# Two attentions and two mixtures of experts on one core: smaller matmul tiles in the first attention, and another way for the gates of the last experts

## The reference

```python
x = layernorm(x + attn0(x))   # causal, scores clipped to [-10, 10], softmax
x = layernorm(x + ffn0(x))    # 8 experts of 256, top 2, silu(x W1) * (x W2) @ W3
x = layernorm(x + attn1(x))   # full attention with rotary q and k, bias on the output
x = layernorm(x + ffn1(x))    # 4 experts of 512, top 2 of softmax(gelu(x rW1) rW2)
# ffn1, the "last experts":
for e in range(4):
    h = gelu((x * mask_e) @ We1[e] + be1[e])
    out += (h @ We2[e] + be2[e]) * weight_e
```

## Time and profile before

| | |
|---|---|
| median of 3 runs | 1720.16 us (1710.94 to 1721.71) |
| profiled execution | 1729.45 us, its span 1727.2 us |
| mean granted TensorE clock | 0.953 of full speed |
| busy: PE, DVE, ACT, POOL | 1566.1, 1410.2, 1167.6, 108.6 us |
| first attention | about 54 to 345 us |
| first experts | about 369 to 744 us |
| second attention | about 790 to 1404 us |
| last experts | about 1428 to 1727 us |

### The profile page before, as it was taken

The page is one execution under the profiler, slowest core; times in us unless marked ns, Lnnn a source line. Parts: engine busy times, 40 slices in busy tenths (PEclk is TensorE's granted clock), DMA queues, the critical chain, the costliest instruction groups (busy, mean ns, idle before and its releaser), DMA issues.

```text
span 1727.2 us, 32148 instructions
## 1 busy us (share of the span) xinstructions
PE 1566.1 (91%) x11104; PEld 801.1 (46%) x11104; DVE 1410.2 (82%) x2503; ACT 1167.6 (68%) x1779; POOL 108.6 (6%) x187
## 2 busy tenths in 40 slices
PE   6899999969999999968999999999999978888887
PEld 3433333346656655633333333333333336666665
DVE  3688999867777777777999999999999827887777
ACT  3798999833333333215999999999999966655565
POOL 2000000000100111020000000000000000010000
PEclk9898999989999999975999999999999989999999
DMA  7482222222322221240111111111111010000100
GB/s 214 146 234 85 91 91 92 69 69 63 100 100 91 71 83 62 91 154 3 44 38 48 54 37 38 37 43 37 42 54 43 18 39 14 20 21 26 34 7 13
DMA packets 68461, 112.97 MB, mean 65 GB/s; under 512 B 23088, under 2 KB 32176, under 8 KB 67712
## 3 DMA queue, kind: packets, MB, share of 16 engines
q1 hardware_dynamic: 68352, 111.48, 20.6%
HBM read 67.79 MB, written 43.65 MB: 65 GB/s over the span
## 4 chain that ended last, share of the span: by engine, by line
PE 57%; DVE 19%; issue 9%; ACT 6%; DMA 4%; SPq 3%; POOL 1%; ACTq 0%; DVEq 0%; POOLq 0%
PE full_o L731 14%; PE max_pair L702 11%; PE causal_o L459 6%; PE hid_pair L1028 6%; PE triple L443 6%; PE score L716 3%; DVE negmax_h L816 3%; PE bank L1119 2%; DVE hid L1435 2%; DVE lin_u L1431 2%; ACT cprobs L487 1%; PE bank L1131 1%; DMA k_scr<-qk_hi 1%; DVE st L1263 1%; PE hid_pair L960 1%
## 5 line engine op out<-in xcount | busy, mean ns | idle before, releaser
L816 DVE TENSOR_REDUCE negmax_h<-max_pair 128x2 f32<-128x1024 f32 x512 | 588.3, 1217 | 23.4 <-PE max_pair L702 23.3
L782 ACT ACTIVATE probs<-score 128x512 f32<-128x512 f32 x1024 | 547.2, 596 | 78.6 <-PE score L716 59.2
L731 PE MATMUL full_o<-probs,v_st 128*32 128x256 f32 x4096 | 330.8, 395 | 17.7 <-ACT o_sb L790 17.7
L716 PE MATMUL score<-q_st,k_st 32*128 32x512 f32 x1024 | 316.6, 503 | 0.8 <-ACT probs L782 0.7
L487 ACT ACTIVATE cprobs<-triple 128x1536 f32<-128x1536 f32 x192 | 265.7, 1454 | 22.6 <-PE triple L443 19.9
L702 PE MATMUL max_pair<-k_st,q_st 32*128 32x512 f32 x1024 | 264.2, 515 | 10.9 <-DVE negmax_h L816 9.6
L1225 ACT ACTIVATE act_s<-hid_pair 128x512 f32<-128x512 f32 x128 | 76.5, 597 | 192.6 <-PE hid_pair L1028 192.5
L702 PEld LDWEIGHTS max_pair<-k_st,q_st 32*128 32x128 f32 x1024 | 97.6, 188 | 234.4 <-DVE negmax_h L816 179.9
L1028 PE MATMUL hid_pair<-x_hi,w_hi 128*128 128x512 f32 x384 | 198.8, 518 | 6.8 <-ACT act_s L1230 6.8
L517 DVE TENSOR_SCALAR cprobs<-cprobs 128x1536 f32<-128x1536 f32 (+6 forms) x272 | 163.5, 625 | 0.4 <-ACT cprobs L487 0.4
L459 PE MATMUL causal_o<-cprobs,v_st 128*32 128x512 f32 (+3 forms) x1536 | 157.6, 507 | 3.2 <-DVE cprobs L517 3.2
(11 more groups left out here) (139 smaller groups left out, 1631.4 us busy)
## 6 DMA issues: line engine op xcount, KB each, us to landing
o_scr<-o_sb SPq DMA_DIRECT2D x64, 256.0 KB, 2.1
gate_all<-gate_scr SPq DMA_DIRECT2D x32, 512.0 KB, 5.6
k_st<-k_scr SPq DMA_DIRECT2D x64, 128.0 KB, 2.8
q_st<-q_scr SPq DMA_DIRECT2D x128, 64.0 KB, 2.4
q_st<-q_scr SPq DMA_DIRECT2D x16, 512.0 KB
k_st<-k_scr SPq DMA_DIRECT2D x64, 104.0 KB
q_scr<-qk_hi SPq DMA_DIRECT2D x24, 256.0 KB, 4.1
k_scr<-qk_hi SPq DMA_DIRECT2D x24, 256.0 KB, 4.2
```

Of the source, the lines that this page charges most:

```text
L716: nc.tensor.matmul(sbank[L.score_bank(e)][:, :], k_st[p][rows, j, kt * P:(kt + 1) * P], q_st[p][rows, q0:q0 + w], start=True, stop=True, t ...
L731: last = nc.tensor.matmul(full_o[SLOT * j:SLOT * (j + 1), cols], v_st[p][:, kt, j, :], probs[s % NP][:, j, cols], start=(kt == 0 and part ...
L782: nc.scalar.activation(probs[s % NP][:, L.HEADS[j], :], sbank[L.score_bank(e)][:, :], ACT.Exp, scale=SCALE).then_inc(L.exp_done, 1)
L816: nc.vector.tensor_reduce(negmax_h[:, qt // TPC, half, heads[0]:heads[1] + 1:2, qt % TPC], ring[slot][:, :, :], AXX, ALU.max, negate=True) ...
```

## The change

- First attention: the keys lie in `k_st[128, T]`, 32 rows for each head, and a score matmul reads 32 rows (`slot_rows`). No zeros are needed. The "twins" pieces pair two key tiles of one head and stand behind key block 0 of the second half, so at most two blocks end in one slot. The first half's output is saved at slot 7, not 5.
- Weights: `w_hi` and `w_lo` have memory of their own and GpSimd makes them, one instruction of 2048 columns a round, in rounds 10 to 13 of the first attention and 2 to 5 of the second. SP loads the weights in rounds 5, 6 and 8 of the first attention, and those of the last experts in the first round of the second. The pad rows are gone; GpSimd fills the two extra key rows with ones by a memset, and fills `v_st`.
- The second attention reads 24 rows (maxima) and 26 rows (scores) of a head. Its first two rounds are loaded during the first experts (chunks 2 and 3).
- Last experts: the gates go to DRAM and back as in the first experts, and are turned in step 2 of their own chunk. Bank 1 becomes the second `y_bank`, and four hidden banks are used. GpSimd makes the router's exponential as a power of e (`pool_gate_exp`, 16 columns), and takes the chunk ahead first. `plan[1]` has other steps, and the first three hidden products stand ahead of the router's second product.
- SP's and GpSimd's loops are written out.

```diff
@@ -50,22 +50,24 @@
-    SAVE_PREV, SAVE_0 = 1, 5
+    SAVE_PREV, SAVE_0 = 1, 7
...
+        twins = [("twins", [(qc, qc * TPC + 2, j, 2 * P * qc, 2 * P) for qc in range(CPB)]) for j in self.HEADS]
         pieces = []
         for qc in range(CPB):
             d = qc * TPC
             for kt in range(d):
                 pieces += [("full", [(qc, kt, j, 0, CH)]) for j in self.HEADS]
+                if kt == 0:
+                    pieces += twins
             pieces += [("first", [(qc, d, j, 0, CH)]) for j in self.HEADS]
             pieces += [("edges", [(qc, d + 3, j, 0, P), (qc, d + 1, j, P, 3 * P)]) for j in self.HEADS]
-            pieces += [("twins", [(qc, d + 2, j, 0, 2 * P), (qc, d + 2, j + 1, 2 * P, 2 * P)]) for j in (0, 2)]
...
-        self.last_kt = [qc * TPC + 2 for qc in range(CPB)]
+        self.last_kt = [2, KT - 1]
...
-        def rows_of(j):
-
-            r = ROWS * (j * SLOT // ROWS)
-            return r, slice(r, r + ROWS)
+        def slot_rows(j, many):
+
+            return SLOT * j, slice(SLOT * j, SLOT * j + many)
...
-                r, rows = rows_of(j)
-                last = nc.tensor.matmul(triple[n % 2][:, bk, off:off + w], k_st[p][rows, j, kt * P:(kt + 1) * P],
+                r, rows = slot_rows(j, SLOT)
+                last = nc.tensor.matmul(triple[n % 2][:, bk, off:off + w], k_st[p][rows, kt * P:(kt + 1) * P],
                                         q_st[p][rows, q0:q0 + w], start=True, stop=True, tile_position=(r, 0))
...
+        def pool_round_weights(layer, k, lower):
+
+            if lower:
+                nc.gpsimd.tensor_tensor(w_lo[k][:, :], w_raw[k][:, :], w_hi[k][:, :].bitcast(F32),
+                                        ALU.subtract).then_inc(w_lower, 1)
+            else:
+                nc.gpsimd.tensor_copy(w_hi[k][:, :], w_raw[k][:, :]).then_inc(w_upper, 1)
+
+        def pool_weights(pool, layer, n):
+
+            k = n // 2
+            if n % 2 == 0:
+                pool.wait_ge(raw_loaded[k], 16 * (layer + 1))
+            else:
+                pool.wait_ge(w_upper, 2 * layer + k + 1)
+            pool_round_weights(layer, k, n % 2 == 1)
+
+        WEIGHTS_FROM = 10
...
+            for i in range(NG - 2):
+                pool.wait_ge(L.pv_done, L.values_before(i + 1))
+                pool_stage_v(pool, L, i + 2, i % 2)
+                if 0 <= i - WEIGHTS_FROM < 4:
+                    pool_weights(pool, 0, i - WEIGHTS_FROM)
+            pool.wait_ge(L.scores_ready, L.N * NG)
+            for p in range(2):
+                nc.gpsimd.memset(k_st[p][:, :].bitcast(F32), 1.0).then_inc(layers[1].ones_set, 1)
...
+            for i in range(4, NG - 2):
+                next_round(i, i % 2)
+                if i == 5:
+                    for t, name in WEIGHTS:
+                        sp.dma_start(t[tuple(slice(None) for _ in t.shape)], d[name]).then_inc(w_loaded, 16)
+                    sp.dma_start(b_o1[:, :], d["b_o1"].broadcast_to([P, D])).then_inc(w_loaded, 16)
+                    sp.dma_start(rb2[:, :], d["rb2"].broadcast_to([P, E1])).then_inc(w_loaded, 16)
+                if i == 6:
+                    for k, name in enumerate(("w1", "w2")):
+                        sp.dma_start(w_raw[k][:, :], d[name]).then_inc(raw_loaded[k], 16)
+                if i == 8:
+                    sp.dma_start(rope_a[:, :], d["rope_a"]).then_inc(rope_loaded, 16)
+                    sp.dma_start(rope_b[:, :], d["rope_b"]).then_inc(rope_loaded, 16)
...
+        def pool_fill_values(pool, L):
+
+            pool.wait_ge(stages[1].y_done, 2 * B * SPC)
             for p in range(2):
-                nc.gpsimd.memset(k_st[p][:, :, :].bitcast(F32), 0.0).then_inc(L.zeroed, 1)
+                nc.gpsimd.memset(v_st[p][:, :, :, :], 0.0).then_inc(fills, 1)
+            pool.wait_ge(fills, FILLS + 4 * L.n + 2)
+            for p in range(2):
+                nc.gpsimd.memset(v_st[p][:, :, :, DK:DK + 1], 1.0).then_inc(fills, 1)
...
+                if 0 <= i - 2 < 4:
+                    pool_weights(pool, 1, i - 2)
...
+            sp.dma_start(w_raw[0][:, :], d["we1"]).then_inc(raw_loaded[0], 16)
+            sp.dma_start(w_raw[1][:, :], d["we2"].rearrange("p n c -> p (n c)")).then_inc(raw_loaded[1], 16)
...
-                          (plan[1], (3, 5, None, None, None, None, 1, 4, 6, 8, 10, 11, 12, 15))):
+                          (plan[1], (4, 6, None, None, None, None, 1, 2, 4, 8, 10, 12, 13, None))):
...
-        h_banks, h_lead = [2, 3], [1, 3]
-
-        y_bank = [bank[0][:, :], hbank[3]]
-        h_of = [[n % 2 for n in range(SPC)], [n % 3 if n < SPC - 1 else 1 for n in range(SPC)]]
-        h_apart = [[2] * SPC, [2 if n in (1, SPC - 1) else 3 for n in range(SPC)]]
+        h_banks, h_lead = [2, 4], [1, 3]
+
+        y_bank = [bank[0][:, :], bank[1][:, :]]
...
-        def pe_gate_rows(pe, st, c, e, layer):
-
-            if e == 0:
-                pe.wait_ge(st.gate_t, c + 1)
-            pe.wait_ge(st.gbc_saved, c * n_exp[layer] + e + 1)
-            nc.tensor.matmul(bank[1][:, :], expert_row[:, e, :], gate_t[:, :], start=True,
-                             stop=True).then_inc(st.gbc_ready, 1)
...
+        def pe_turn_gates(pe, st, f):
+
+            pe.wait_ge(st.gates, f + 1)
+            for t in range(TPC):
+                last = nc.tensor.transpose(bank[3][0:E0, slice_of(t)], gts[:, 0, t, :], ident[:, :])
+            last.then_inc(st.gates_turned, 1)
...
-                pe_gate_step(pe, st, c, n, layer)
+                if layer == 1 and n == GATES_AT:
+                    pe_turn_gates(pe, st, c)
...
+                if layer == 1 and n == plan[1].hidden:
+                    pe_first_hidden(pe, st, layer)
...
-                        nc.scalar.activation(e_sm[:, :, :], sc8[:, :, 0:E1], ACT.Exp).then_inc(st.gate_exp, 1)
...
+        def act_save_gates(act, st, f):
+
+            act.wait_ge(st.gates_turned, f + 1)
+            wait_used(act, st.gates_kept, 16 * f)
+            nc.scalar.activation(gate_rows[:, :], bank[3][0:E0, :], ACT.Copy).then_inc(st.gate_t, 1)
...
+                    if n == GATES_AT + 1:
+                        act_save_gates(act, st, c)
...
-            dve.wait_ge(st.gbc_saved, 1 + c * E1 + e + 1)
+            dve.wait_ge(st.gate_in[e // 2], 16 * (c + 1))
...
+        def pool_gate_exp(pool, st, f):
+
+            pool.wait_ge(st.gate_pre, f + 1)
+            nc.gpsimd.tensor_tensor(e_sm[:, :, :], euler[:, :].rearrange("p (t e) -> p t e", e=E1), sc8[:, :, 0:E1],
+                                    ALU.pow).then_inc(st.gate_exp, 1)
+
+        def pool_front(pool, pc, st, f, layer):
+
+            pool_rstd(pool, pc, st.stats, st.rstd, 0, f + 1)
+            if layer == 1:
+                pool_gate_exp(pool, st, f)
+
         def pool_end(pool, st, layer):
             pc = Chain(pool, st.pool_chain)
-            for c in range(2):
-                pool_rstd(pool, pc, st.stats, st.rstd, 0, c + 1)
-
-            with pool.Fori(0, 2 * B - 2) as c:
-                pc.at(2 + 2 * c)
-                if layer == 0:
+            for f in range(2):
+                pool_front(pool, pc, st, f, layer)
+            for c in range(2 * B):
+                if c + 2 < 2 * B:
                     pool_rstd(pool, pc, st.stats, st.rstd, 0, c + 3)
+                if layer == 0 and c == 2 * B - 1:
+                    pool_fill_values(pool, layers[1])
                 pool_back(pool, pc, st, c, layer)
-                if layer == 1:
-                    pool_rstd(pool, pc, st.stats, st.rstd, 0, c + 3)
-            for c in (2 * B - 2, 2 * B - 1):
-                if layer == 0 and c == 2 * B - 1:
-                    pool_clear_full(pool, layers[1])
-                pc.at(2 + 2 * (2 * B - 2) + c - (2 * B - 2))
-                pool_back(pool, pc, st, c, layer)
+                if layer == 1 and c + 2 < 2 * B:
+                    pool_gate_exp(pool, st, c + 2)
...
+                if c in (2, 3):
+                    sp.wait_ge(layers[1].ones_set, 2)
+                    sp_load_full(sp, layers[1], c - 2, c - 2)
...
+            keep_gates(st, 0)
+            load_gates(st, 0, range(E1 // 2))
+            for c in range(-1, 2 * B):
+                f = min(c + 3, LAST)
+                if c >= 0:
                     store_out(c)
-                    sp_load_o(sp, st, layers[1], c + 3, b + 1 + hh, 1 - hh)
-            for c in range(B, 2 * B):
-                f = min(c + 3, 2 * B - 1)
-                if c + 3 <= 2 * B:
-                    sp_load_sums(sp, st, layers[1], c + 3, f // 2, f % 2)
-                store_out(c)
-                if c + 3 < 2 * B:
+                if c + 3 <= LAST:
                     sp_load_o(sp, st, layers[1], f, f // 2, f % 2)
+                f = min(c + 4, LAST)
+                if c + 4 <= LAST + 1:
+                    sp_load_sums(sp, st, layers[1], c + 4, f // 2, f % 2)
+                if c + 2 <= LAST:
+                    keep_gates(st, c + 2)
+                    load_gates(st, c + 2, range(E1 // 2))
```

(14 more changed lines are left out.)

251 lines of the change are left out of this document (74 added, 177 removed).

## The result

The changed kernel takes 1997.68 us (median of 4 runs, 1995.25 to 2001.72) where the kernel before took 1720.93 in the same session: a ratio of 1.162, 95% interval [1.158, 1.166]. I had forecast 1688, and faster.

A forecast was written before the change was run, and what follows sets the result against it. Bounds taken: ScalarE in the first attention, VectorE's maxima in the second, TensorE's order in the last experts. Sum: -6.0 - 5.6 + 7 - 1.5 - 1.0 + 1.0 - 26 = -32, from 1720.16 to 1688 us; range 1660 to 1714.

The forecast's parts named there:

- The second attention is bound by VectorE's maxima over PSUM, which the change does not touch.: Second attention: VectorE was taken as the bound, with no gain or loss from reading fewer rows.
- the prediction is wrong if the clock falls in the first attention: Sign against the forecast: TensorE's granted clock falling in the first attention; no such sign was named for the second.
- Part 1: First attention's loads: moving weight loads and dropping pad stores removes a 6.5 us stall; -6.0 us (ends -6.5 and 0).
- Part 2: First attention's 32-row tiles and new piece order: half of 0.7 us a round, -5.6 us (ends -10.4 and 0).
- My rival that small tiles change nothing: First attention: waits of 0.7 us a round stay; -26.5 us in all, so 1694 us; chance 0.08.
- Part 3: First attention: GpSimd's rounding of weights, 16 us in four instructions, holds VectorE; +7 us (ends 0 and +16).
- part 4: Between the stages: -1.0 and -0.5 us around the attentions, -1.0 at the last experts' head, +1 for second-attention loads.
- +1.0 for the second attention: Second attention's first round: new weight loads stand ahead of the next round's maxima rows; +1 us (ends 0 and +4).
- Part 5: Last experts' chunks: less work on TensorE and ScalarE, exponential on GpSimd; period 34.0 us, -26 us (ends -9 and -42).
- 29.54 - 0.4 + 1.56 + 2.5 = 33.2 us: VectorE's floor per last-experts chunk: busy time, less removed operations, plus small gaps and the wait for GpSimd's power.
- My first rival: VectorE stays the late one: last experts' period only 36.5 us, GpSimd holds VectorE 16 us; 1714 us; chance 0.15.
- the -26 of the last experts: Last experts: 6 x 3.8 = 22.8 us from shorter chunks, plus 3 for the first and last chunk.

The follow-up runs named there:

- b_order: Kernel before with only the first attention's new order of pieces and sums saved in slot 7, tiles still of 64 rows: 1715.75 us, ratio 0.998.
- a32: Changed kernel with the second attention's maxima and scores both reading all 32 rows of a head again: 1709.81 us, ratio to before 0.993.

## Why the prediction was wrong

**The step that failed** stands in its first paragraph: "The second attention is bound by VectorE's maxima over PSUM, which the change does not touch." The change does touch the stage, by reading 24 and 26 rows instead of 32. I took that for a cut of nothing. It keeps TensorE at 1.2 GHz, where its instructions fill 897.5 of 900 us and VectorE's 603; at the higher level they had been 593.9 and 562.1 of 614. I had written that the prediction is wrong if the clock falls in the first attention; there, with 32 full rows, it did not, and I had no such rival for the second. The sign was in the trace of before: that stage begins at 0.50 and rises only some 22 us later. A stage that begins at the low level depends on rising, so a change of its matmuls' shape should have been a rival with the whole stage at stake. Why rows that are not read keep the clock down, no run here shows.

Part 1 held: no round of the changed kernel has the stall of before, 6.5 us. Part 2 was too small. "ScalarE can win at most 17.3 - 16.61 = 0.7 us a round" took the busy time of the exponentials as fixed. They take 1.35 us back to back and more one by one, so a round fell to 16.2, and 1.1 x 16 = 18 us came instead of 5.6. My rival that small tiles change nothing falls, and b_order shows that the order alone doesn't do it. Part 3 had the right mechanism and a short price: 10 us for the two subtractions alone instead of 7 for all four. The rule that it cites from the Trainium skill, "GPSIMD Engine Reference", Key points, agrees with the trace: the two-input clip was held for the whole 4.5 us. Together -6.5 - 18 + 10 = -14.5, and the stage lost 14.0. Of part 4's 2.5 us nothing is to be seen: the stretches between the stages have their old lengths, and from the second attention's last values' product to TensorE's first router product it is 11.4 us in a32 and 11.3 before. Its +1.0 for the second attention and GpSimd's four instructions there don't show either: from the first scores to the last values' product the stage is 4.3 us longer in a32, and its clock rose some 15 us later, which is worth about that much.

Part 5 had every operation nearly right: the power 3.13 us for 3.5, VectorE's wait 2.1 for 2.5, the gate rows in time. What failed is the sum behind "29.54 - 0.4 + 1.56 + 2.5 = 33.2 us". It left out the 5.3 us that VectorE stood for ScalarE, as if they went with the table loads, and put "three steps of lead cover most of that; I take 34.0" in their place. 4.8 of them stayed: 29.54 - 0.4 + 1.56 + 2.1 + 4.8 = 37.6, and the period became 37.5. Some 2 us of them hang on the order of steps (`ot`, the gates' turn, the gate rows, `act_s`), some 1.3 on the power itself, as the experiments show; for the rest no run was made. My first rival ("VectorE stays the late one", 36.5) named the result and not these waits. With the exponential and the projection put elsewhere the stage gives 24.8 us by the windows, near the 26 that I forecast for it, but by two changes that the prediction didn't have.

Leaving the clock out, a32 is the change as I had pictured it: 1709.8 us, inside my range and 22 above my 1688. That it is inside is no proof of the sum: nearly all of what it wins is won in the first attention, and the -26 of the last experts didn't come at all.

## What to carry to other kernels

A tile that leaves rows idle costs no time by itself (the fastest maxima took 490 ns with 24 rows and 489 with 32) and can cost the clock: before cutting rows of zeros, look at whether the stage starts at the lower level and must climb out. When one cause of a wait goes, don't take the whole wait out of the sum: follow the engine that is waited for, in its own order of work, and see what else stands ahead of the result. Long two-input operations of GpSimd beside a busy VectorE belong in pieces that VectorE's slack covers.

## What was new about the hardware

The granted clock did not follow TensorE's busy share. With tiles of 24 and 26 rows it stood at 0.50 while TensorE was busy 897.5 of 900 us, and rose within 4 us once only the 128-row products of the values were left. With 32 rows in both, some of them zeros in the queries, it rose to 1.00 after 23 us in the kernel before and 39 in a32, at busy shares of 0.95 to 1.00. With one of the two kinds at 32 rows the rise came after some 148 and 204 us and lasted. The Trainium skill, "TensorE: Matmul & The Clock Gate", Part 1, says that the gate sets the clock by how busy TensorE has been recently; this case's traces do not agree where busy is taken as time, and the measurement decides. Which row count is enough was not tried.

GpSimd's power on 16 columns takes 3.13 us and on 4 columns 1.02 to 1.62, so it goes mostly by column. Its copy of 2048 columns takes 1.89 us, its subtraction 4.54. ScalarE's table load of 1.28 us and an exponential of 0.21 are quicker than that power.
